# Attention stacks loaded two groups at a time in halves of heads, and the maxima scores begun a quarter step earlier

## The reference

```python
x = x + xattn(layernorm(x), ctx, pos)     # softmax(q k^T / 4) v, then Wout and bias
x = x + ffn(layernorm(x))                 # 512 -> 2048 -> gelu -> 512, weights cut to -g, 0, g
# logits = einsum('bqhd,bkhd->bhqk', q, k) * scale ; w = softmax(logits)
```

## Time and profile before

| what | value |
|---|---|
| median of three runs | 773.16 us (772.75 to 773.92) |
| the profiled execution's own time | 771.07 us |
| its span | 769.3 us |
| PE busy | 754.0 us, 98% |
| DVE busy | 661.9 us, 86% |
| ACT busy | 481.9 us, 63% |
| POOL busy | 430.1 us, 56% |

### The profile page before, as it was taken

One profiled execution on the slowest core, in us unless ns is written; L12 is line 12 of the kernel. 1 busy time (PEld: TensorE's weight loads), 2 busy tenths in 40 slices (PEclk: granted clock), 3 DMA queues, 4 the chain that ended last, 5 costly groups with the idle time before them and its releaser, 6 DMA issues.

```text
span 769.3 us, 11882 instructions
## 1 busy us (share of the span) xinstructions
PE 754.0 (98%) x3886; PEld 342.9 (45%) x3886; DVE 661.9 (86%) x927; ACT 481.9 (63%) x830; POOL 430.1 (56%) x501
## 2 busy tenths in 40 slices
PE   5999999999999999999999999999999999999998
PEld 3887877333323322332233223345554455555443
DVE  7888999788888888889888888479998889998895
ACT  4787766787788777788878888765323433333330
POOL 5787776675345446456446557665564845564310
PEclk9999999999999999999999999999999999999999
DMA  8588996555587778887777896326566575544655
GB/s 279 176 219 249 267 260 167 138 141 132 139 170 147 152 157 138 161 179 144 151 162 162 180 192 154 73 69 136 116 135 124 101 147 114 119 96 96 114 106 136
DMA packets 178862, 117.24 MB, mean 152 GB/s; under 512 B 119746, under 2 KB 150514, under 8 KB 178802
## 3 DMA queue, kind: packets, MB, share of 16 engines
q1 hardware_dynamic: 178802, 116.49, 67.6%
HBM read 64.50 MB, written 25.43 MB: 117 GB/s over the span
## 4 chain that ended last, share of the span: by engine, by line
PE 87%; DMA 4%; DVE 2%; ACT 2%; POOL 2%; SPq 1%; issue 1%; POOLq 0%; DVEq 0%; ACTq 0%
PE banks L741 15%; PE banks L725 14%; PE banks L1040 14%; PE banks L1025 14%; PE banks L702 12%; PE banks L297 8%; PE banks L1006 6%; DMA stack_words<-max_rows 2%; PE banks L328 1%; DMA max_rows<-max_parts 1%; PE banks L713 1%; SPq L619 1%; PE banks L280 1%; SPq L257 1%; POOL attn_words L527 0%
## 5 line engine op out<-in xcount | busy, mean ns | idle before, releaser
L815 ACT ACTIVATE probs_words<-banks 128x512 f32<-128x512 f32 x512 | 290.7, 596 | 70.7 <-PE banks L725 57.9
L795 DVE TENSOR_REDUCE maxima<-banks 128x2 f32<-128x1024 f32 x240 | 283.2, 1216 | 41.4 <-PE banks L702 41.4
L725 PE MATMUL banks<-stack_words 98*128 98x512 bf16 x512 | 173.6, 382 | 2.2 <-DMA stack_words<-max_rows 1.2
L702 PE MATMUL banks<-stack_words 96*128 96x512 bf16 x480 | 143.0, 379 | 0.0
L741 PE MATMUL banks<-probs_words,late_words 128*32 128x512 f32 x1024 | 136.4, 605 | 0.0
L725 PEld LDWEIGHTS banks<-stack_words 98*128 98x128 bf16 x512 | 48.7, 96 | 158.0 <-ACT probs_words L815 109.1
L1025 PE MATMUL banks<-ternary_words,late_words 128*128 128x512 f16 x512 | 113.1, 379 | 0.0
L1040 PE MATMUL banks<-ternary_words,stack_words 128*128 128x512 f16 x512 | 112.9, 379 | 0.0
L1224 ACT ACTIVATE probs_words<-probs_words,h_moments 128x2048 f32<-128x2048 f32 (+1 forms) x17 | 32.2, 1901 | 120.6 <-DVE h_moments L1103 120.6
L826 POOL TENSOR_SCALAR neg_max<-maxima 128x16 f32<-128x16 f32 x32 | 8.3, 260 | 145.4 <-DVE maxima L795 145.4
L1025 PEld LDWEIGHTS banks<-ternary_words,late_words 128*128 128x128 f16 x512 | 49.8, 98 | 60.5 <-issue 0.8
(11 more groups left out here) (157 smaller groups left out, 1065.2 us busy)
## 6 DMA issues: line engine op xcount, KB each, us to landing
o_rows<-late_words SPq DMA_DIRECT2D x32, 256.0 KB, 3.4
k_parts<-ternary_words SPq DMA_DIRECT2D x48, 128.0 KB, 3.0
q_parts<-ternary_words SPq DMA_DIRECT2D x48, 128.0 KB, 2.5
stack_words<-q_parts SPq DMA_DIRECT2D x32, 192.0 KB, 3.2
stack_words<-k_parts SPq DMA_DIRECT2D x96, 64.0 KB, 2.7
stack_words<-k_parts SPq DMA_DIRECT2D x32, 192.0 KB, 2.7
attn_words<-in_x_dram SPq DMA_DIRECT2D x16, 256.0 KB, 4.0
probs_words<-in_L_ffn_w_fc_dram SPq DMA_DIRECT2D x16, 256.0 KB, 3.6
```

What stands on the lines that cost most here:

```text
L702: mm = self.nc.tensor.matmul(self.score_slot[j % 2][:, i], self.mem.q_stack[0:STACK, slot, head, c * P:(c + 1) * P], self.mem.k_stack[0:ST ...
L725: self.nc.tensor.matmul(self.st_bank[(g * 16 + k) % self.ST_BANKS], self.mem.k_stack[0:STACK + 2, slot, head, c * P:(c + 1) * P], self.mem ...
L795: dve.tensor_reduce(self.maxima[:, g % 2, 2 * j:2 * j + 2], self.score_slot[j % 2], AX.X, ALU.max).then_inc(self.scores_read, 1)
L815: act.activation(self.probs[:, c, head, :], self.st_bank[(g * 16 + k) % self.ST_BANKS], ACT.Exp, scale=1 / math.sqrt(HEAD)).then_inc(self. ...
```

## The change

**Loading.** A load now covers a pair of groups (2p, 2p+1) and half of the heads: lower (heads 0, 1) in SP's iteration 2p-1, upper (heads 2, 3) in iteration 2p. The stacks have six slots; the third pair of slots lies in `late_words`. A DMA takes rows of both groups, 2 KB each, where it took rows of one group, 4 KB each. The lower half has rows 0 to 95, the upper half rows 16 to 111; the other 16 rows are zero, and ones and maxima move to rows 112 and 113. A half takes 7 (lower) or 8 (upper) DMAs. The zeros are written once by two DMAs in phase 1, from a row that POOL sets, and the third pair's zeros and ones by three DMAs at the start of phase 2.

**Scores.** A pair is now one chunk of a lower head and the same chunk of an upper head (rows 0:96 and 0:112), instead of two chunks of one head. Pairs are issued `LEAD` = 2 ahead: step s holds pairs 2 to 7 of group s and pairs 0 and 1 of group s+1, the last two in quarter 3.

```diff
+LEAD = 2
+Q_RUNS = (((0, 0, 1), (1, 0, 3), (4, 1, 1), (5, 0, 1)), ((0, 0, 3), (3, 0, 1), (4, 0, 2)))
+K_RUNS = (((0, 0, 2), (2, 0, 1), (3, 0, 3)), ((0, 2, 1), (1, 1, 1), (2, 0, 1), (3, 0, 2), (5, 0, 1)))
...
-    def load_stacks(self, sp, g):
-        mem, slot = self.mem, g % STACK_SLOTS
-        for pair in range(2):
-            sp.wait_ge(self.prj.parts_stored[pair], PAIR_STORES * (g // HG + 1))
-        need(sp, self.st_ready, (g - STACK_SLOTS + 1) * 16)
...
+    def load_stacks(self, sp, pair, half):
+
+        mem, g = self.mem, 2 * pair
+        for i in range(2):
+            sp.wait_ge(self.prj.parts_stored[i], PAIR_STORES * (g // HG + 1))
+        need(sp, self.st_ready, (g - 2 * STACK_PAIRS + 2) * 16)
+        for t, where, runs in ((0, mem.q_parts, self.Q_RUNS[half]), (1, mem.k_parts, self.K_RUNS[half])):
+            src = where[g:g + 2].rearrange("g t (d h) c -> (t d) g (h c)", h=GH)
             for to, part, count in runs:
...
     def scores(self, pe, g, j):
-        head, slot = j // 2, g % STACK_SLOTS
-        if j == 0:
-            pe.wait_ge(self.stacks_loaded[slot], (g // STACK_SLOTS + 1) * STACK_LOADS)
+
+        if j == 0 and g % 2 == 0:
+            for half in range(2):
+                self.wait_stacks(pe, g, half)
...
         need(pe, self.scores_read, (g - self.EARLY) * 2 * GH + j - 1)
...
-            begun = s == self.EARLY and c == 0
+            begun, ahead = s == self.EARLY and c == 0, s * 2 * GH + 2 * c + self.LEAD
             if 0 <= turned < GROUPS and not begun:
                 self.scores_turned(pe, turned, 4 * c)
-            if s < GROUPS and not begun:
-                self.scores(pe, s, 2 * c)
+            if not begun:
+                self.scores_ahead(pe, ahead)
...
-            if s < GROUPS and not begun:
-                self.scores(pe, s, 2 * c + 1)
+            if begun:
+                self.scores_ahead(pe, ahead)
+            self.scores_ahead(pe, ahead + 1)
...
+                if s == 4:
+                    prj.clear_rows(sp, att.rows_set)
...
                 if s == 2:
+                    att.begin_late_stacks(sp)
+                    att.load_stacks(sp, STACK_PAIRS - 1, 0)
                     for pair in range(2):
                         sp.wait_ge(prj.parts_stored[pair], PAIR_STORES * BATCH)
                 if s == 3:
-                    att.load_stacks(sp, STACK_SLOTS)
+                    att.load_stacks(sp, STACK_PAIRS - 1, 1)
                     att.turn_max(sp, 2)
                     att.load_max(sp, 2)
...
-                if STACK_SLOTS < s < GROUPS:
-                    att.load_stacks(sp, s)
+                if 2 * STACK_PAIRS <= s + 1 < GROUPS:
+                    att.load_stacks(sp, (s + 1) // 2, (s + 1) % 2)
...
-                    if j == 1 and s >= 3:
+                    if j == 3 and s >= 3:
                         att.save_sums(dve, s - 3)
...
+            pool.wait_ge(prj.piece_ready[1], 4)
+            pool.memset(prj.row_zeros, 0.0).then_inc(prj.row_ones_set, 1)
```

More of the change, by code:

```diff
@@ L27 @@
 PARTS = 3
-STACK = 6 * HEAD
+MAX_ROW = 7 * HEAD
+STACK = MAX_ROW + 2
 AXES, FREQS = 2, 4
@@ L39 @@
 STACK_SLOTS = 4
-STACK_LOADS = DMA * 7
+STACK_PAIRS = 3
+STACK_LOADS = (DMA * 7, DMA * 8)
 INPUT_SLOTS = 4
@@ L568, in __init__ @@
         self.st_bank = [banks[:, 4 + i] for i in range(self.ST_BANKS)]
-        self.stacks_loaded = [sem(f"stacks_loaded_{i}") for i in range(STACK_SLOTS)]
+        self.stacks_loaded = [[sem(f"{half}_stacks_loaded_{i}") for i in range(2)] for half in ("lower", "upper")]
         self.max_loaded = [sem(f"max_loaded_{i}") for i in range(STACK_SLOTS)]
@@ L604, in early_of, with stack_pair @@
         return list(range(first, first + self.PER_STEP[at]))
-    def load_stacks(self, sp, g):
-        mem, slot = self.mem, g % STACK_SLOTS
-        for pair in range(2):
-            sp.wait_ge(self.prj.parts_stored[pair], PAIR_STORES * (g // HG + 1))
-        need(sp, self.st_ready, (g - STACK_SLOTS + 1) * 16)
[L613 to L617, removed]
-            for to, part, count in runs:
-                sp.dma_start(stack_sb[to * HEAD:(to + count) * HEAD, slot].rearrange("p h c -> p (h c)"),
-                             src[part * HEAD:(part + count) * HEAD]).then_inc(self.stacks_loaded[slot], DMA)
+    def stack_pair(self, t, pair):
+        r = pair % STACK_PAIRS
+        if r == STACK_PAIRS - 1:
+            return self.late_stacks[:, t]
+        return (self.mem.q_stack, self.mem.k_stack)[t][:, 2 * r:2 * r + 2]
@@ new lines, in stack, with begin_late_stacks @@
+    def stack(self, t, g):
+        return self.stack_pair(t, g // 2)[:, g % 2]
+    def begin_late_stacks(self, sp):
+        late = self.late_stacks.rearrange("p t s h c -> p (t s) h c")
+        for first, heads in ((MAX_ROW - HEAD, slice(0, 2)), (0, slice(2, 4))):
+            rows = slice(first, first + HEAD)
+            sp.dma_start(late[rows, :, heads].rearrange("p n h c -> p n (h c)"),
+                         self.mem.k_stack[rows, :, heads].rearrange("p n h c -> p n (h c)")).then_inc(self.rows_set, DMA)
+        rows = slice(MAX_ROW, MAX_ROW + 2)
+        sp.dma_start(self.late_stacks[rows, 1].rearrange("p s h c -> p (s h) c"),
+                     self.mem.k_stack[rows, 0:2].rearrange("p s h c -> p (s h) c")).then_inc(self.rows_set, DMA)
@@ new lines, in load_stacks @@
+    def load_stacks(self, sp, pair, half):
[5 more added lines that the diff above has]
+            src = where[g:g + 2].rearrange("g t (d h) c -> (t d) g (h c)", h=GH)
+            for to, part, count in runs:
+                row = (to + half) * HEAD
+                sp.dma_start(self.stack_pair(t, pair)[row:row + count * HEAD, :, 2 * half:2 * half + 2].rearrange(
+                                 "p s h c -> p s (h c)"),
+                             src[part * HEAD:(part + count) * HEAD, :, half * 2 * SEQ:(half + 1) * 2 * SEQ]
+                             ).then_inc(self.stacks_loaded[half][pair % 2], DMA)
```

60 lines of the change are left out of this document (40 added, 20 removed).

## The result

| | before | after |
|---|---|---|
| median | 772.95 us (771.33 to 773.92, 4 runs) | 779.83 us (777.24 to 781.98, 4 runs) |
| profiled execution | 771.07 us, span 769.3 | 777.24 us, span 775.4 |
| ratio | | 1.0086 (95%: 1.0058 to 1.0115) |

The change makes the kernel 0.9% slower. A second measurement, beside other experiments, gave 1.0083 (1.0060 to 1.0106). The forecast was 773.9 us, no change; 779.8 lies outside its range. Both profiled executions are quicker than the median of their kernel, by 1.9 and 2.6 us.

A forecast was written before the change was run, and what follows sets the result against it. TensorE was taken to bound phase 2's steady state, DVE close behind. Terms -1.9 +1.4 +0.7 +0.8 -0.4 +0.2 = +0.8 on the profiled 771.07 gave 771.9; the median, 2.1 higher, 773.9 us (8 in 10: 771.3 to 777.0).

The forecast's parts named there:

- the start: Start of phase 2: two more score pairs ahead of the first PV move it from 144.21 to 145.6, +1.4 us.
- the maxima: Middle of phase 2: maxima written a quarter sooner remove all TensorE waits for them, -1.9 us.
- the end: Step 31, end of phase 2: one more quarter loses a pair and shortens from 2.84 to 2.40, -0.4 us.
- phase 1: POOL's zeroing of a 512-column row delays work TensorE's transposes wait on: +0.2 us, between 0 and 0.5.
- The third pair of slots: +0.7: Upper-half load of groups 4 and 5 lands at 162.3, wanted by pair 0 of group 4 at 161.6: +0.7 us.
- hidden behind the first two delays, with nothing to spare: Maxima of group 2, queued behind groups 4 and 5's upper half, land by 164.9, wanted at 165.0: no added wait.
- The upper halves, +0.8: Steady state, quarter 3 of odd steps: two or three TensorE waits for upper-half loads, 0.3 to 0.6 each, +0.8 us.
- Rows 96 against 98 make no difference in their pace, so I expect none from 112 and 114.: Phase 2 matmuls: the new contraction heights leave the regular quarter at 2.84 us, no change.
- Rival (a): Start costs more: first upper half lands after 5.0 us, wait 3.0, maxima of group 2 follow; 776.2 us, chance 0.2.
- (b): SP's issues become the bound: 0.69 us per stack DMA, upper halves 2.6 us later; 794 us, chance 0.08.
- (c): Start of phase 2 is free and stacks are never waited for: 771.0 us, faster, chance 0.12.
- (d): Upper half lands sooner by a better spread of DMA targets, no waits for stacks: 772.4 us, chance 0.15.

The follow-up runs named there:

- Experiment 2: The kernel before with only the earlier scores (`LEAD` = 2) on the old loads: 771.79 us, ratio 0.9987.
- experiment 9: The kernel before plus only the memset of a zero row and the two DMAs that spread it in phase 1: 773.38 us, ratio 1.0002.
- Experiment 7: The changed kernel with eleven more filler matmuls ahead of pair 0 of group 4: 777.47 us, ratio 1.0058 to the kernel before.
- experiments 3: The changed kernel with the upper half of groups 4 and 5 issued right behind the lower half: 778.5 us, ratio 1.0068 to the kernel before.
- experiment 4: The changed kernel with pairs of two chunks of one head, as before the change: 775.32 us, ratio 1.0035 to the kernel before.
- experiment 5: The changed kernel with a pair being one chunk of both heads of one half: 776.42 us, ratio 1.0037 to the kernel before.
- experiment 6: The changed kernel with pairs of one head and group 2's maxima turned ahead of groups 4 and 5's upper half: 772.69 us, ratio 0.9991 to the kernel before.
- experiment 1: The changed kernel with `LEAD` = 0, new loads but scores where they were before: 784.1 us, ratio 1.0148 to the kernel before.

## Why the prediction was wrong

- **Right:** the start (+1.4 for 1.37, the pair waiting for DVE at the place named), the maxima (-1.9 for -1.88), the end (-0.4 for -0.44), issues of 0.42 us, the place and the tile of the wait near 161.6. Experiment 2 confirms the first three, with a start of 1.37, no late maxima and two quarters of 2.40.
- **Right by luck:** phase 1, +0.2 for 0.25. Its end moves by more than that from one execution to the next (1.57 us between the two traces of the changed kernel). The late maxima are near this: 1.9 in the trace that was read, 5.1 in that of experiment 9, so -1.9 holds for the pair of traces compared.
- **The step that failed most** is "The third pair of slots: +0.7". Its queue was right to 0.5 us (160.0 for 159.5), and in part by luck: `load_max(1)` ended 0.5 sooner than before, and the three DMAs of zeros and ones took 2.0 us for the 1.4 reckoned. The landing was taken from a quiet iteration, 2.7 us, and was 4.3 to 4.8. The earlier trace rows was the exception and not the rule: in ten of the 13 even iterations from 178 us on in the kernel before, the stacks took 3.5 us or more to land, in three 2.4 to 3.1. Three of the ten, from the views of L619 over 223 to 227, 315 to 319 and 428 to 432 us:

```profile
DMA to landing us min/median/max: 3.8/4.1/4.1
...
DMA to landing us min/median/max: 3.9/4.2/4.4
...
DMA to landing us min/median/max: 3.7/3.9/3.9
```

  The loads at the very place of the change, from 152.8 us, did take 2.5 to 3.2 before. There seven DMAs were issued in this stretch; now fifteen follow one another, and the DMA share of 155 to 160 us is 1.11 where it was 0.45. Whether their number, their shorter rows or the other traffic makes the landing long is open. I had written as the bound, 3.0 us of wait, and 2.74 lies inside it. Outside of it lies the lower clock behind the wait, 1.42 us, which the text did not think of. Experiment 7 shows it.
- In the same step, "hidden behind the first two delays, with nothing to spare" was put too mildly. Without the stall the maxima of group 2 are late by 1.7 to 2.7 us (experiments 3, 4 and 5): the 4.18 us stood ahead of a second wait, and only experiment 6 removed both.
- **The upper halves, +0.8:** the mechanism was right, TensorE waiting in quarter 3 of odd steps; the size was 1.7 to 2.7 us. In the trace of the change the five late ones are the upper halves that took 4.1 to 5.4 us to land; the other eight took 4.0 or less. Experiment 4 takes the waits all away.
- **"Rows 96 against 98 make no difference in their pace, so I expect none from 112 and 114."** The rows as such make none (experiment 4). Mixed within a pair they cost 6.6 ns a quarter, 0.7 us (experiment 5). The earlier trace rows could not show this, since no pair there had two heights.
- Rival (a) had the right mechanism, a landing as in the earlier trace rows and the maxima of group 2 behind it, at a chance of 0.2, and 776.2 us, which is 774.2 for the profiled execution. With the clock (1.4), the pace (0.7) and the larger upper halves (1.2), less 0.3 of wait, it comes to the 777.2 measured there. (b) is refuted by the issues of 0.42, (c) by the start, (d) by the landings: in the trace of the change the upper half of groups 4 and 5 took 4.3 to 4.8 us to land where the lower half, seven DMAs earlier and in a less loaded queue, took 3.1 to 4.1, and the upper halves of the 13 later iterations took 2.6 to 5.4, where whole groups took 2.4 to 5.1 in the same iterations before. By the table of ports in the Trainium skill ("SBUF — State Buffer", the section on the DMA port swizzle) rows 16 to 111 reach all 16 ports, as rows 0 to 95 do, and in both cases the fullest port has eight of the rows, so the page gave no reason to expect a faster landing. No run here separates ports.

## What to carry to other kernels

A block of transfers that is put in front of a deadline should be priced with the landing time of a loaded queue, and the wait behind it in the same queue has to be priced as if the first one did not exist. Ask of a wait of some us on TensorE also what clock the work behind it gets: here 2.74 us of wait cost 4.2, and filler in the stall kept the clock up. Where an operation is moved earlier to gain room, move it by as little as the lateness needs: one pair (1.42 us) covered waits of at most 0.94 for 0.14 us, two pairs cost 1.37. And read the landings of every iteration before one of them is taken for the sum.

## What the runs showed of the hardware

- In phase 2 the granted clock stayed 1.00 behind idle times of TensorE of 2.19 us (experiment 4) and 2.30 us (experiment 1, at 312.7 us) and fell around those of 2.51, 2.58, 2.89 and 4.66 us (experiment 5, the changed kernel twice, experiment 1; 0.50 over 5 us in the last, which is 1.2 GHz). These are single traces and no limit: in six of the eight executions of experiment 4 the mean granted clock was 0.995 to 0.998, so it fell in them too, and in two of the ten executions of the changed kernel it was 1.000, with 776.92 and 780.29 us.
- The windows print a granted clock of 1.00 for the start of the program as well, and the rows there say otherwise. The same two matmuls, in the changed kernel at 10.70 and at 24.85 us:

```profile
10.70 1.05 PE L308 MATMUL banks<-wk_high,ctxT_low 128*128 128x512 f32 x2
...
24.85 0.63 PE L308 MATMUL banks<-wk_high,ctxT_low 128*128 128x512 f32 x2
```

  From start to start they are 427 and 230 ns apart. The faster pace begins at 14.1 us here and at 21.0 in the kernel before, so the 1.00 given for its whole execution holds from there on, but for the last microsecond.
- Behind two bf16 matmuls of 512 columns with one height of contraction the next matmul, of another height, started after 215 ns (98 behind 96; 114 behind 96 or 112). Where the two had 96 and 112, it started after 218.
